# Moving 17 of 40 source one-hots from VectorE to ScalarE in a graph layer with experts

## What is computed

```python
def rgcn_conv(x, edge_index, edge_type, W_rel, W_root, bias):
    src, dst = edge_index                       # 20000 edges among 625 nodes
    out = x @ W_root + bias
    for r in range(2):
        w = (edge_type == r)
        sums = segment_sum((x[src] @ W_rel[r]) * w, dst)
        out = out + sums / maximum(segment_sum(w, dst), 1)
    return out
x = x + (h + elu(rgcn_conv(rms_norm(h), ...)) @ wo)   # h = layernorm(x), itself added to x
x = x + experts(layernorm(x))                         # 2 shared, 8 routed, top 2
```

## Time and profile before

| | |
|---|---|
| median of 3 runs | 346.65 us (346.63 to 348.71) |
| the profiled execution | 347.6 us, span 345.9 us |
| busy: TensorE, VectorE, ScalarE | 321.4, 236.6, 131.2 us |
| TensorE's granted clock | 1.00 in all parts of the span |
| edge loop | from about 31 to 83 us |

### The profile page before, as it was taken

The page is one execution under the profiler, slowest core; times in us unless marked ns, Lnnn a source line. Parts: engine busy times, 40 slices in busy tenths (PEclk is TensorE's granted clock), DMA queues, the critical chain, the costliest instruction groups (busy, mean ns, idle before and its releaser), DMA issues.

```text
span 345.9 us, 5736 instructions
## 1 busy us (share of the span) xinstructions
PE 321.4 (93%) x1904; PEld 277.1 (80%) x1904; DVE 236.6 (68%) x461; ACT 131.2 (38%) x175; POOL 71.6 (21%) x91
## 2 busy tenths in 40 slices
PE   0799998888999999989998999999999999999995
PEld 0699897667789888878997888888888888878873
DVE  2999999996774582972746748665645656571994
ACT  2668142042013215161318655555644555530000
POOL 5643110000101101020022222342122320003840
PEclk9999999999999999999999999999999999999999
DMA  8960022000001015759122387499798992124994
GB/s 247 329 178 3 0 92 77 2 1 2 14 3 61 2 61 182 244 158 380 64 83 101 95 294 278 137 338 380 257 322 285 366 374 99 69 116 147 318 333 168
DMA packets 26753, 57.59 MB, mean 167 GB/s; under 512 B 2701, under 2 KB 16281, under 8 KB 26724
## 3 DMA queue, kind: packets, MB, share of 16 engines
q1 hardware_dynamic: 20198, 33.89, 29.0%
q0 software_dynamic: 3888, 14.16, 12.4%
q10 hardware_dynamic: 2638, 9.17, 6.8%
HBM read 66.25 MB, written 14.03 MB: 232 GB/s over the span
## 4 chain that ended last, share of the span: by engine, by line
PE 68%; DVE 12%; ACT 7%; issue 6%; DVEq 3%; DMA 3%; POOL 0%; SPq 0%; ACTq 0%
PE ps L1317 35%; PE ps L1582 16%; PE ps L1428 5%; PE ps L1572 4%; DVE work L963 4%; DMA raw<-in_L_gnn_W_rel 3%; PE ps L1327 2%; ACT arena_r L692 2%; DVEq L976 2%; DVE sw_raw L963 1%; PE ps L1463 1%; DVE big L973 1%; PE ps L1590 1%; ACT tile L699 1%; ACT arena_r L751 1%
## 5 line engine op out<-in xcount | busy, mean ns | idle before, releaser
L1317 PE MATMUL ps<-arena_r 128*128 128x512 f32 (+1 forms) x264 | 67.3, 401 | 0.2 <-DVE arena_r L1047 0.2
L1582 PE MATMUL ps<-big,tile 128*128 x272 | 61.7, 380 | 1.1 <-ACT tile L812 1.0
L1317 PE MATMUL ps<-arena_r,xt 128*128 128x286 f32 (+1 forms) x360 | 60.2, 311 | 0.3 <-ACT raw L708 0.3
L1317 PE MATMUL ps<-xt,arena_r 128*128 128x314 f32 (+2 forms) x312 | 59.6, 343 | 0.2 <-DVE xt L1038 0.2
L1582 PEld LDWEIGHTS ps<-big,tile 128*128 128x128 f32 x272 | 51.4, 190 | 9.3 <-issue 1.8
L1317 PEld LDWEIGHTS ps<-arena_r 128*128 128x128 f32 (+1 forms) x264 | 48.0, 188 | 11.0 <-DVE arena_r L1047 0.6
L1317 PEld LDWEIGHTS ps<-xt,arena_r 128*128 128x128 f32 (+1 forms) x312 | 50.2, 187 | 6.4 <-DVE xt L1038 0.4
L603 POOL DMA_INDIRECT big<-xrow,tok_i x17 | 31.6, 1857 | 99.7 <-PE ps L1572 75.4
L1317 PEld LDWEIGHTS ps<-arena_r,xt 128*128 128x128 f32 (+1 forms) x360 | 50.9, 194 | 1.2 <-ACT raw L708 0.5
L842 ACT ACTIVATE arena_r<-raw 128x2048 fp32r x17 | 32.5, 1910 | 26.7 <-DMA raw<-in_L_ffn_W 16.7
L1246 DVE TENSOR_TENSOR arena_r<-raw,arena_r 128x2048 fp32r<-128x2048 f32 x17 | 38.8, 2283 | 2.0 <-ACT arena_r L842 2.0
(11 more groups left out here) (210 smaller groups left out, 358.2 us busy)
## 6 DMA issues: line engine op xcount, KB each, us to landing
big<-in_L_ffn_W SPq DMA_DIRECT2D x19, 1024.0 KB, 7.7
raw<-in_L_ffn_W SPq DMA_DIRECT2D x19, 1024.0 KB, 10.2
yrow<-work ACTq DMA_DIRECT2D x17, 512.0 KB, 3.4
raw<-in_L_gnn_W_rel SPq DMA_DIRECT2D x2, 1144.0 KB, 12.0
y_acc<-in_x SPq DMA_DIRECT2D x4, 512.0 KB, 8.4
xrow<-work SPq DMA_DIRECT2D x4, 512.0 KB, 2.9
raw<-in_L_ffn_sW SPq DMA_DIRECT2D x2, 1024.0 KB, 5.9
sw_raw<-in_L_ffn_sW SPq DMA_DIRECT2D x2, 1024.0 KB, 12.5
```

What stands on the lines that cost most here:

```text
L1317: ins = pe.matmul(out_ap, a, b, start=start and k == 0, stop=stop and k == n - 1)
L1582: ins = pe.matmul(ps[1][:, i % 2, 0:HID], xg_t[:, k * P:(k + 1) * P], big[:, bass.ds(ring * UNIT + k * HID, HID)], start=k == 0, stop=k == ...
```

## The change

The source one-hots of groups 7, 9, 11, ... 39 (17 groups) are made by ScalarE. Step one, src_distance: four Abs activations give |column number - lo| with the negated lo as bias, one for each of the 4 columns of edges, 128 elements each, read and written as f16 with a stride of two. Step two, src_hots: one Relu over all 512 elements in place gives max(0, 1 - distance), which is exactly 1 or 0. The Abs of the next of these groups stand in front of the Relu of this one. The negated lo is made once (160 elements). VectorE leaves out its comparison in these groups. TensorE waits for ScalarE's one-hots there too. In ScalarE's queue the new work lies between split_rows(4) and the h_out's, and the five add_normed stand behind everything, after unit_hi(4).

```diff
+        ACT_HOT = tuple(range(7, G, 2))
+            neg_lo = in_t
+            def src_distance(i):
+                g = ACT_HOT[i]
+                if g >= N_SH:
+                    act.wait_ge(s_cnt, g - N_SH + 1)
+                for c in range(CG):
+                    ins = act.activation(src_hot[g % N_SH][:, c // 2, :, c % 2], iota_s[0:CE, :, 0], ACT.Abs,
+                                         bias=neg_lo[:, g, c:c + 1])
+                ins.then_inc(s_dist, 1)
+            def src_hots(i):
+                act.wait_ge(s_dist, i + 1)
+                hot = src_hot[ACT_HOT[i] % N_SH]
+                act.activation(hot, hot, ACT.Relu, bias=1.0, scale=-1.0).then_inc(s_shot, 1)
+            def act_hots(first, last):
+                for i in range(first, last):
+                    src_distance(i + 1)
+                    src_hots(i)
             h_out(0)
             split_rows(3, 3)
+            act.wait_ge(s_grp, 1)
+            act.activation(neg_lo, lo_t, ACT.Copy, scale=-1.0).then_inc(s_neg, 1)
+            act.wait_ge(s_neg, 1)
             h_out(1)
+            src_distance(0)
+            act_hots(0, 3)
             split_rows(4, 4)
-            act.wait_ge(s_rows, 1)
-            add_normed(0)
-            for t in range(2, T):
-                h_out(t)
-                add_normed(t - 1)
-            add_normed(T - 1)
+            act_hots(3, 4)
+            h_out(2)
+            act_hots(4, 7)
+            h_out(3)
+            act_hots(7, 15)
+            h_out(4)
+            act_hots(15, len(ACT_HOT) - 1)
+            src_hots(len(ACT_HOT) - 1)
             act.wait_ge(s_small, 32)
             act.activation(rw_hl[:, :, 0, :], rw_sb[:, :, :], ACT.Copy).then_inc(s_rw, 1)
             unit_hi(3)
             unit_hi(4)
+            act.wait_ge(s_rows, 1)
+            for t in range(T):
+                add_normed(t)
...
-                compare(src_hot[n % N_SH], iota_s, lo)
+                if both:
+                    compare(src_hot[n % N_SH], iota_s, lo)
...
-                    hots(g, lo_t[:, g, :], v_t[:, g, :]).then_inc(s_hot, 1)
+                    hots(g, lo_t[:, g, :], v_t[:, g, :], g not in ACT_HOT).then_inc(s_hot, 1)
...
                 pe.wait_ge(s_hot, g + 1)
+                if g in ACT_HOT:
+                    pe.wait_ge(s_shot, act_hots_upto(g))
```

More of the change, by code:

```diff
@@ L301, in program @@
         s_hot = sem("s_hot")
+        s_neg = sem("s_negated")
+        s_dist = sem("s_distance")
+        s_shot = sem("s_srchot")
         s_cnt = sem("s_counted")
@@ L635, in steps_of, with act_hots_upto @@
             return h_steps[upto(g):upto(g + 1)]
+        ACT_HOT = tuple(range(7, G, 2))
+        def act_hots_upto(g):
+            return sum(1 for a in ACT_HOT if a <= g)
         def count_bank(n):
@@ L957, in _, with hots @@
             stats_x(4)
-            def hots(n, lo, key):
+            def hots(n, lo, key, both=True):
                 def compare(hot, columns, index):
```

## The result

The changed kernel takes 342.21 us (median of 4, 341.74 to 342.75) against 346.64 before: 4.43 us less, a ratio of 0.986 with a 95% interval of 0.9826 to 0.9894. A second set of runs gave 342.20 against 346.71, 0.9864 (0.9839 to 0.9889). The forecast was 341.65.

A forecast was written before the change was run, and what follows sets the result against it. VectorE was taken to pace the loop (1.09 us per group, TensorE 0.79). 5.70 saved less 0.65 stall and 0.05 at the end gave 5.0: profiled 347.6 becomes 342.6, median 0.95 lower, 341.65 us; range 340.6 to 344.8.

The forecast's parts named there:

- VectorE's saving, 17 x 0.335 = 5.70: In the loop, VectorE skips 17 source one-hots of 0.335 us; a pair of groups then takes it 1.85 us.
- The stall at the addition of group 8, 0.65: VectorE waits 0.65 us for count(8), late behind group 7's 33 matmuls on TensorE.
- VectorE's sequencer: Per group in the loop, load, register work and assertion were put under 0.6 us, so not limiting.
- ScalarE's price, 1.79 us: One moved group on ScalarE: four Abs at 0.294 plus a Relu at 0.614 us; bounds 1.63 and 2.27.
- Is it fast enough, and where does ScalarE take over?: ScalarE's loop queue keeps up; takes over at 1.87 us per group, slope 15, gain gone at 2.20.
- The rule of the Trainium skill that relu belongs on VectorE: Read as busy time, it would turn 5.7 us saved into 30 spent; decides only if ScalarE paces.
- What is moved is hidden: The rw copy, unit_hi(3), (4) and five add_normed run later on ScalarE, hidden by 4.7 and 6.9 us.
- The gain goes through: Behind the loop nothing has a fixed time, so the full 5.0 us reaches the end; lost later 0.05.
- table loads: Rival: Abs or Relu bring a 1.28 us table load on ScalarE, count(7) about 1.0 late, 342.6; chance 0.03.
- f16 at a stride does not halve the rate: Denies the rival of ScalarE taking f16 at half rate: 2.64 us per group, 353.2 us; chance 0.05.
- neighbours overlap: Denies the rival of no overlap between ScalarE instructions: 2.27 us per group, 347.6 us; chance 0.05.
- ScalarE as pace-maker: Rival: ScalarE partly paces the loop at 1.87 to 2.20 us per group; 343.6 at 2.0; chance 0.15.

The follow-up runs named there:

- run 3: Changed kernel with only nine groups (23, 25, ... 39) on ScalarE instead of 17: 343.89 us, ratio 0.9909; loop 2.90 us shorter than before the change.
- the repeat: The changed kernel itself, timed and profiled again: 342.20 us, loop 40.55 us.
- run 10: Changed kernel with groups 34 and 38 also on ScalarE (nineteen), h_out(4) behind all of them: 341.82 us, ratio 0.9838, loop 40.19 us.
- Run 8: Changed kernel with one or two extra Abs per ScalarE group, into unused memory: 343.91 us (loop +1.63) and 347.99 us (loop +6.06).
- run 2: Changed kernel with the source one-hots of groups 9, 11, ... 39 made by nobody: 342.01 us, ratio 0.9856, loop 40.53 us.
- runs 4 and 5: Kernel before with only add_normed moved: 347.42, again 346.93 us; changed kernel without one-hots of groups 9 to 39 (odd), add_normed at old places: 342.22 us.
- runs 6 and 9: Changed kernel with all five add_normed back in the loop: 346.22 us; with groups 34 and 38 also on ScalarE, h_out(4) before the last five: 344.82 us.

## Why the prediction was right, point by point

- **VectorE's saving, 17 x 0.335 = 5.70.** Right: a pair takes 1.85 us, and nine groups alone give 0.32 each (run 3).
- **The stall at the addition of group 8, 0.65.** Right: from start to start it costs 47.17 - 46.01 - 0.485 = 0.67 (the idle time of 0.59 in the row leaves out the overlap of neighbours), and 0.65 is what the first eight groups lack in run 3.
- **The loop, 5.0 shorter.** It is 4.93 (4.92 in the repeat).
- **VectorE's sequencer, "under 0.6 us, below both beats".** Wrong, and without effect. The durations of the long instructions were added up, but one round of the sequencer takes 0.85 us (the last section shows it). That is more than VectorE's 0.76 and TensorE's 0.79 in an odd group. It did no harm because the even group takes 1.09: two rounds are 1.71 us, a pair 1.85. In run 10, where groups on ScalarE are neighbours, it sets the pace.
- **ScalarE's price, 1.79 us.** 0.10 too high, all of it in the Relu. The Abs stand 1.17 / 4 = 0.293 apart, against 0.294 from line 692. The Relu was priced with the fixed part of an instruction that has a pointer operand, 0.187 from start to start; its bias and scale are constants, and it takes 0.52, so 0.52 - 0.427 = 0.09 fixed. The measured duration of 0.617 (mean of the 17) is within 1% of what the Trainium skill gives ("ScalarE: Activation LUTs", section "What ACT_TABLE_LOAD costs": 186 ns and 0.833 ns per element, 93 ns more for a pointer operand, 93 ns of overlap between neighbours); by it the Relu comes to 0.613, 0.520 from start to start.
- **Is it fast enough, and where does ScalarE take over?** Right in both: no wait of TensorE for ScalarE, and 15 us per us of excess from 1.87 on. Run 8 hit both points within 0.1 us. The margin at the end was larger than thought, for group 37 2.2 us instead of 0.8. The first Relu ended at 40.48 for a count at 40.97, 0.5 to spare instead of 0.3.
- **The rule of the Trainium skill that relu belongs on VectorE** ("ScalarE: Activation LUTs", section "Rules for kernel authors") is met in its premise, a ScalarE that is slower at it (1.69 against 0.335 us per group), and was without effect on the time: run 2 shows the 27 us to cost nothing.
- **What is moved is hidden.** Right, by runs 4 and 5. The Exp had 8.29 us in front of it; 6.9 was said.
- **The gain goes through.** 4.43 of 4.93 by the medians. The missing 0.5 lies inside the interval of the ratio (3.7 to 6.0 us) and inside the scatter of the parts in front of and behind the loop, in which no experiment found an effect of the change. It stays open whether it is more than chance.
- **The rivals.** The changed kernel has the same two table loads as the kernel before, neither of them in the loop, f16 at a stride does not halve the rate, and neighbours overlap. ScalarE as pace-maker was the real one: the kernel is 0.2 us per group away from it.

## What to carry to other kernels

Moving work to a slower engine pays as long as that engine keeps up with the beat of the one relieved: work out its price from start to start, the price at which it takes over, and the slope beyond, since the change from gain to loss here takes only 0.5 us per group. An in-order queue must hold nothing that is not urgent in front of urgent work, and nothing that waits for a late event (runs 6 and 9); the same move is worth nothing when the engine is idle. Look for the tightest item of the queue, which need not be the last one. Price an engine's sequencer by the distance of its rounds, not by the sum of its durations. Read a changed stage by its own length between two rows, when the parts around it scatter by a microsecond.

## What the runs showed of the hardware that I had not expected

- After a pause of 2.24 us, with TensorE busy for 0.87 of the 3 us up to 78, its granted clock stood at 0.50 for some 3 us, and a beat took 1.4 us instead of 0.79. The pause of 1.74 us in the same execution (from 59.97 on) left it at 1.00, as did 1.75 in the kernel with three add_normed inside and 1.20 in that with two more Abs. So a late producer can cost more than its lateness.
- An Abs of 128 f16 elements lasts 393 ns where its output is contiguous (line 746) and 431 where it has a stride of two (line 749), but they follow each other at the same distance: one more Abs made a group 0.29 us dearer. The longer duration is not a price.
- VectorE's two-instruction groups run at 0.76 us when a three-instruction group stands in front, but groups 34 and 35 of run 10, in a row of three, at 0.85, though the counts that they add had ended over half a microsecond before. The limit is VectorE's sequencer. Its rows in that kernel (duration in ns min/median/max, first and last start):

```profile
L1019 DVEq TENSOR_LOAD <-d_i x6: 301/302/307, 69.2 to 73.5; - x6
...
L1016 DVEq FUSED_REGOPS  x3: 52/52/52, 69.0 to 70.7; - x3
L1016 DVE TENSOR_TENSOR big<-big,ps x3: 363/364/366, 69.1 to 70.8; 128x200 f32 x3
```

The loads of the run-time position come every (73.5 - 69.2) / 5 = 0.86 us, the register work for the address of an addition every (70.7 - 69.0) / 2 = 0.85, and each of these additions starts 0.1 behind it. Groups 37 and 38 run at 0.76 again, since group 36 with its 1.09 us lets the sequencer get ahead by 0.24.
